# Slot attention: two batches run as two streams half a round apart

## What is computed

```python
Pn = rmsnorm(P, input_norm_w)
k_proj, v_proj = Pn @ Wk.T, Pn @ Wv.T
for _ in range(3):
    sn = rmsnorm(slots, slot_norm_w)
    q_proj = sn @ Wq.T
    scores = jnp.einsum('bkd,bmd->bkm', q_proj, k_proj) * SCALE
    attn = jax.nn.softmax(scores, axis=-2)
    attn = attn / (jnp.sum(attn, axis=-1, keepdims=True) + EPS)
    updates = jnp.einsum('bkm,bmd->bkd', attn, v_proj)
    slots = gru_cell(updates, slots, wih, whh, bih, bhh)
```

## Time and profile before

| What | us |
|---|---|
| Runs (three) | 3412.17, 3408.17, 3413.89 |
| Median | 3412.17 |
| The profiled execution, its own time | 3412.49 |
| Its span, from the first to the last instruction | 3410.7 |
| PE busy in it | 2470.1 (72%) |
| DVE busy | 2040.2 (60%) |
| ACT busy | 1425.7 (42%) |
| Mean granted clock of TensorE | 0.843 of full speed |

### The profile page before, as it was taken

How to read it: one execution, slowest core, us unless ns; L and a number is a source line. 1 busy time by engine, 2 the same in 40 slices (tenths; PEclk the granted TensorE clock), 3 DMA queues, 4 the chain that set the end, 5 groups by cost and what they waited for, 6 DMA issues and landing times. The chain is left out here.

```text
span 3410.7 us, 37710 instructions
## 1 busy us (share of the span) xinstructions
PE 2470.1 (72%) x12065; PEld 1570.8 (46%) x12066; DVE 2040.2 (60%) x4897; ACT 1425.7 (42%) x2245; POOL 423.8 (12%) x228
## 2 busy tenths in 40 slices
PE   2999995363666666654799277877884996899598
PEld 1444443241333333323799145545433884454387
DVE  4666662857777777733465345565654556675377
ACT  1555551113888777861344122122351222266121
POOL 0000000011000000001675120211100111200021
PEclk8999998675777777766899689988886997799799
DMA  1001102043011111001564200000521111531010
GB/s 59 21 24 25 26 17 78 17 131 96 1 26 26 26 26 26 7 1 47 181 202 145 80 0 0 0 0 11 149 51 34 45 31 64 156 86 32 30 42 31
DMA packets 87781, 174.61 MB, mean 51 GB/s; under 512 B 23560, under 2 KB 52240, under 8 KB 84176
## 3 DMA queue, kind: packets, MB, share of 16 engines
q1 hardware_dynamic: 86096, 168.64, 16.9%
q0 software_dynamic: 1536, 4.20, 0.4%
HBM read 133.41 MB, written 38.99 MB: 51 GB/s over the span
## 5 line engine op out<-in xcount | busy, mean ns | idle before, releaser
L1497 ACT ACTIVATE l1a_over_s<-l1a_sc_s,l1a_minus_step_s 128x1024 bf16<-128x1024 f32 x256 | 290.0, 1140 | 3.0 <-DVE l1a_minus_step_s L1371 1.7
L1311 DVE MAX8 l1a_cand_s<-ps 128x8 f32<-128x128 f32 x1024 | 213.2, 282 | 69.0 <-PE ps L1206 65.1
L1239 PE MATMUL ps<-l1a_probs_s,l1h_v_s 128*32 128x256 f32 x1024 | 123.3, 570 | 159.8 <-ACT l1a_probs_s L1505 158.5
L1483 ACT ACTIVATE l1a_sc_s<-ps,l1a_minus_tau_s 128x1024 f32<-128x1024 f32 x128 | 142.0, 1112 | 140.3 <-DVE l1a_minus_tau_s L1340 53.1
L1024 DVE TENSOR_REDUCE l3a_shift_s<-ps 128x1 f32<-128x1024 f32 x128 | 150.1, 1219 | 51.1 <-PE ps L941 51.1
L1206 PE MATMUL ps<-l1h_ka_s,l1h_qa_s 128*128 128x512 f32 x256 | 132.2, 559 | 56.1 <-DVE l1a_cand_s L1311 45.5
L1085 ACT ACTIVATE l3a_probs_s<-ps 128x512 f32<-128x512 f32 x256 | 132.7, 603 | 88.9 <-PE ps L957 88.7
L1962 PE MATMUL ps<-m1e_x_part_s,m1e_up_part_s 128*128 128x256 f32 x1152 | 151.7, 289 | 13.6 <-POOL m1e_up_part_s L2142 12.0
L1962 PEld LDWEIGHTS ps<-m1e_x_part_s,m1e_up_part_s 128*128 128x128 f32 x1152 | 144.4, 196 | 17.0 <-POOL m1e_up_part_s L2142 15.0
L1505 ACT ACTIVATE l1a_probs_s<-ps 128x1024 f32<-128x1024 f32 x128 | 125.7, 1016 | 62.7 <-PE ps L1227 62.7
L646 ACT ACTIVATE l0a_probs_s<-ps 128x1024 f32<-128x1024 f32 x128 | 124.1, 1021 | 53.6 <-PE ps L482 52.0
(11 more groups left out here) (575 smaller groups left out, 5509.8 us busy)
## 6 DMA issues: line engine op xcount, KB each, us to landing
m1e_up_s<-m_up SPq DMA_DIRECT2D x32, 768.0 KB, 4.4
m1e_down_s<-m_down SPq DMA_DIRECT2D x16, 768.0 KB, 4.6
l1h_ka_s<-l_k_parts SPq DMA_DIRECT2D x16, 512.0 KB, 8.0
l3h_ka_s<-l_k_parts SPq DMA_DIRECT2D x16, 512.0 KB, 8.0
l0a_w_s<-l_w SPq DMA_DIRECT2D x16, 384.0 KB, 3.1
m3ew_up_s<-m_up SPq DMA_DIRECT2D x6, 768.0 KB, 4.3
l0a_rden_s<-l0a_rden_rows SPq DMA_DIRECT2D x32, 128.0 KB, 2.9
m_sorted<-ones SPq DMA_DIRECT2D x1, 4096.0 KB, 16.5
```

The lines of the kernel that those rows point to most:

```text
L1239: ins = nc.tensor.matmul(ps[32 * h:32 * h + 32, VALUES, 0:HALF], v[:, n % 2, t, h, :], probs[:, t % 4, h * HALF:(h + 1) * HALF], start=(t ...
L1311: ins = nc.vector.max(cand[:, r, 8 * (c + j * 4):8 * (c + j * 4) + 8], ps[:, A0 + f % 2, c * P:(c + 1) * P])
L1483: nc.scalar.activation(sc[:, r, :], ps[:, PAIR + 2 * (place % 2):PAIR + 2 * (place % 2) + 2, :].rearrange("p a n -> p (a n)"), ACT.Relu, b ...
L1497: nc.scalar.activation(over[:, done % 2, :], sc[:, r, :], ACT.Relu, bias=minus_step[:, r:r + 1], accum_out=total[:, i, r:r + 1]).then_inc( ...
```

## The change

The loop over three rounds is written out as six phases h, where phase h belongs to batch h % 2 and round h // 2. Between the chunks of phase h stand the last three updates, the denominator, the gates and the new state of phase h-1, and then the queries of phase h+1, which is the same batch as h-1. Score banks are 0 and 1 alone, updates 2 and 3, the gates r, z, xn, hn in 4 to 7; queries use 4 and 5, square sums 6, denominators 7. The gates' products with the slots (`state_gates`) are issued apart from those with the updates (`update_gates`), and each gate has semaphores of its own. Squares are made by VectorE instead of ScalarE. The last phase turns batch 0 before the gates of batch 1. The diff, cut:

```diff
     ITERS = 3
+    PHASES = ITERS * B
-    LAG = 3
-    FIRST, SECOND = (0, 1, 5, 6), (2, 3, 4, 7)
+    SCORES, UPDATE, DEN = 0, 2, 7
+    R, Z, XN, HN = 4, 5, 6, 7
+    QUERIES, SQUARES = 4, 6
...
+        def tokens(h):
+            return slice(h % B * NQ, h % B * NQ + NQ)
+
+        def queries_in(h):
+            return 1 <= h and h + 1 < PHASES
...
         @block.tensor
-            with pe.Fori(0, ITERS) as i:
...
+            def scores(h, t):
+                k = NC_ * h + t
+                if t == 0:
+                    pe.wait_ge(q_ready, KC * h + KC)
+                if k >= 2:
+                    pe.wait_ge(exp_done, k - 1)
+                at = (h % B * NC_ + t) * P
+                product(SCORES + k % 2, k_parts, slice(at, at + P), qu_parts, tokens(h)).then_inc(scored, 1)
...
+            def denominator(h):
+                pe.wait_ge(attn_summed, NC_ * h + NC_)
+                if h > 0:
+                    pe.wait_ge(hn_read, KC * h)
+                nc.tensor.matmul(ps[:, DEN, :], ones[:, :], attn_sum[:, :], start=True, stop=True
+                                 ).then_inc(den_made, 1)
...
+            def state_gates(h, m):
+                u = KC * h + m
+                if u > 0:
+                    pe.wait_ge(r_done, u)
+                product(R, weights["whh"], gate(0, m), slot_parts, tokens(h), last=False)
+                pe.wait_ge(den_read, h + 1)
+                if u > 0:
+                    pe.wait_ge(hn_read, u)
+                product(HN, weights["whh"], gate(2, m), slot_parts, tokens(h))
+                if u > 0:
+                    pe.wait_ge(z_done, u)
+                product(Z, weights["whh"], gate(1, m), slot_parts, tokens(h), last=False).then_inc(whh_made, 1)
+
+            def update_gates(h, m):
+                u = KC * h + m
+                pe.wait_ge(upd_ready, h + 1)
+                product(R, weights["wih"], gate(0, m), qu_parts, tokens(h), first=False).then_inc(r_made, 1)
+                if u > 0:
+                    pe.wait_ge(hn_ready, u)
+                product(XN, weights["wih"], gate(2, m), qu_parts, tokens(h)).then_inc(n_made, 1)
+                product(Z, weights["wih"], gate(1, m), qu_parts, tokens(h), first=False).then_inc(z_made, 1)
...
+            for h in range(B):
+                if h > 0:
+                    pe.wait_ge(mean_ready, h)
+                    pe.wait_ge(q_ready, KC * h)
+                square_sums(h)
+                queries(h)
+            for h in range(PHASES):
+                scores(h, 0)
+                if h > 0:
+                    update(h - 1, 5)
+                scores(h, 1)
+                if h > 0:
+                    update(h - 1, 6)
+                    denominator(h - 1)
+                    update(h - 1, 7)
+                scores(h, 2)
+                scores(h, 3)
+                if h > 0:
+                    state_gates(h - 1, 0)
+                    update_gates(h - 1, 0)
+                update(h, 0)
+                if h > 0:
+                    state_gates(h - 1, 1)
+                    update_gates(h - 1, 1)
+                update(h, 1)
+                scores(h, 4)
+                if queries_in(h):
+                    square_sums(h + 1)
+                update(h, 2)
+                scores(h, 5)
+                if queries_in(h):
+                    queries(h + 1)
+                update(h, 3)
+                scores(h, 6)
+                update(h, 4)
+                scores(h, 7)
+            h = PHASES - 1
+            update(h, 5)
+            update(h, 6)
+            denominator(h)
+            update(h, 7)
+            turn(0)
+            for m in range(KC):
+                state_gates(h, m)
+                update_gates(h, m)
+            turn(1)
...
         @block.scalar
+            for h in range(PHASES):
+                for t in range(4):
+                    exponential(h, t)
+                if h > 0:
+                    for m in range(KC):
+                        gates(h - 1, m)
+                if queries_in(h):
+                    root(h + 1)
+                for t in range(4, NC_):
+                    exponential(h, t)
...
         @block.vector
+            def state(h, m):
+                u, tok = KC * h + m, tokens(h)
+                more = h + B < PHASES
+                dve.wait_ge(n_ready, u + 1)
+                own.link(nc.vector.tensor_tensor(slots[:, m, tok], slots[:, m, tok], n_t[:, u % 2, :], ALU.subtract))
+                dve.wait_ge(z_done, u + 1)
+                own.link(nc.vector.tensor_tensor(slots[:, m, tok], slots[:, m, tok], z_t[:, u % 2, :], ALU.mult))
+                nc.vector.tensor_tensor(slots[:, m, tok], slots[:, m, tok], n_t[:, u % 2, :], ALU.add
+                                        ).then_inc(state_done, 1)
+                dve.wait_ge(state_done, u + 1)
+                if more:
+                    own.done(nc.vector.tensor_tensor(sq[:, m, :], slots[:, m, tok], slots[:, m, tok], ALU.mult))
+                    if m == KC - 1:
+                        own.wait()
+                        nc.vector.sem_inc(sq_ready, 1)
+                    dve.wait_ge(whh_made, KC * h + KC)
+                    cut(m, tok, parts_ready)
...
+            for h in range(PHASES):
+                largest(h, 0)
+                if h > 0:
+                    attention(h - 1, 7)
+                largest(h, 1)
+                attention(h, 0)
+                if h > 0:
+                    finish(h - 1)
+                largest(h, 2)
+                attention(h, 1)
+                largest(h, 3)
+                attention(h, 2)
+                if h > 0:
+                    candidate(h - 1, 0)
+                attention(h, 3)
+                if h > 0:
+                    state(h - 1, 0)
+                    candidate(h - 1, 1)
+                    state(h - 1, 1)
+                largest(h, 4)
+                if queries_in(h):
+                    means(h + 1)
+                largest(h, 5)
+                if queries_in(h):
+                    roots_over(h + 1)
+                attention(h, 4)
+                if queries_in(h):
+                    queries(h + 1)
+                largest(h, 6)
+                attention(h, 5)
+                largest(h, 7)
+                attention(h, 6)
```

More of the change, by code:

```diff
@@ L2567, in slot_gru @@
         sq = s.sb("sq", [P, KC, BANK])
-        rs = s.sb("rs", [P, 2, BANK])
-        dev = s.sb("dev", [P, BANK])
+        rs, dev = s.sb("rs", [P, BANK]), s.sb("dev", [P, BANK])
         top = s.sb("top", [P, 8])
@@ new lines, in _ @@
+            act.wait_ge(b_ready, 1)
+            for h in range(B):
+                root(h)
+            for h in range(PHASES):
+                for t in range(4):
+                    exponential(h, t)
+                if h > 0:
+                    for m in range(KC):
+                        gates(h - 1, m)
[3 more added lines that the diff above has]
+                    exponential(h, t)
+            for m in range(KC):
+                gates(PHASES - 1, m)
@@ new lines, in add @@
+            def add(b):
+                dve.wait_ge(turned, b + 1)
+                for t4 in range(2 * b, 2 * b + 2):
+                    rows = x[:, 2 * t4:2 * t4 + 2, :].rearrange("p a n -> p (a n)")
+                    nc.vector.tensor_tensor(rows, rows, ps[:, t4, :], ALU.add).then_inc(added, 1)
+            for h in range(B):
+                if h > 0:
+                    dve.wait_ge(sq_summed, h)
+                for m in range(KC):
+                    own.done(nc.vector.tensor_tensor(sq[:, m, :], slots[:, m, tokens(h)], slots[:, m, tokens(h)], ALU.mult))
+                own.wait()
+                nc.vector.sem_inc(sq_ready, 1)
+                for m in range(KC):
+                    cut(m, tokens(h), parts_ready)
+                if h == 0:
+                    dve.wait_ge(loaded, 32)
+                    nc.vector.tensor_tensor(brz[:, :], bih[:, 0:4], bhh[:, 0:4], ALU.add).then_inc(b_ready, 1)
+                means(h)
+                roots_over(h)
+                queries(h)
@@ L2832, in _ @@
+            h = PHASES - 1
+            attention(h, 7)
+            finish(h)
+            add(0)
+            for m in range(KC):
+                candidate(h, m)
+                state(h, m)
+            add(1)
+            dve.wait_ge(added, 4)
         @block.gpsimd
         def _(pool):
-            with pool.Fori(0, ITERS) as i:
-                for k in range(CHUNKS):
-                    b, t = divmod(k, NC_)
-                    if t == 0:
-                        continue
+            for h in range(PHASES):
+                for t in range(1, NC_):
+                    k = NC_ * h + t
+                    pool.wait_ge(attn_ready, k + 1)
```

351 lines of the change are left out of this document (141 added, 210 removed).

## The result

| | before | after |
|---|---|---|
| Median of four runs each, us | 3410.47 (3408.17 to 3413.89) | 3360.62 (3354.55 to 3362.88) |
| The profiled execution, its own time | 3412.49 | 3360.47 |
| Its span | 3410.7 | 3358.5 |
| The stage, from its first load to that of the next stage | 384.76 | 329.47 |
| PE, DVE, ACT busy | 2470.1, 2040.2, 1425.7 | 2464.4, 2048.2, 1425.8 |

The ratio is 0.9848 [0.9835, 0.9862]: faster, by 50 us in the medians and 52 in the two profiled executions. The forecast was 3359.1 us.

The account below looks back on a forecast made before the run. The prediction took uncovered latencies of one batch as the bound, 90 of 376 us being waiting or low clock. Stage -59.2, holds +2.4 and clock +3.4 made -53.4 from 3412.5: 3359.1 us, 80% range 3339 to 3381.

Parts of the forecast that it names:

- The finish hidden by the state gates: In a steady phase, VectorE's 7.63 us finish is ready at 14.95, before TensorE's state gates end at 15.8.
- A phase: Steady phases 1 to 4: 47.1 us of TensorE work plus new waits of 1.5 and 1.6 us, 50.2 us.
- Named waits: TensorE waits 1.5 us for the squares and 1.6 us for exponential 6 before the next phase's first scores.
- GpSimd's holds: VectorE operations held beside GpSimd additions: query casts 0.6 us per phase, 2.4 us in all; bounds 0 and 10.8.
- The clock: TensorE's clock falls after idle gaps: two falls taken, 3.4 us; bounds none and ten gaps, 17 us.
- Ends: Stage start and finish: first maximum at 2012.6, phase 5 takes 75.5 us, stage ends at 2309.8 instead of 2368.96.
- Busy sums: Sign: VectorE's busy sum unchanged but for moved squares, 12 x 0.69, replacing 6.4 us of ScalarE's.
- The sum: Whole program: stage -59.2, holds +2.4, clock +3.4, together -53.4 us, giving 3359.1 us.
- (A): Rival: TensorE-bound, both new waits vanish through quicker VectorE hand-overs; phase 47.1 us, time 3341 us; chance 0.13.
- (B): Rival: VectorE's order bounds, with held operations, growing gaps and clock falls; phase 56.3 us, time 3377 us; chance 0.20.
- (C): Rival: slower, TensorE stays at the low clock in interleaved phases; at a third of the work 3432 us; chance 0.04.
- (D): Rival: no overlap, late finish delays update gates, 12 us more in each of five phases; about 3412 us; chance 0.03.

Follow-up runs that it names:

- e1_seq: Kernel after the change, but each phase does its own updates, gates and next queries before the other stream's first chunk: 3411.21 us, ratio 0.9993.
- e9_three: Kernel after the change with early reciprocal, tanh ahead of z and earlier first queries of the second stream, square sum kept first: 3346.35 us, ratio 0.9799.
- e3: Kernel after the change without six of GpSimd's seven running additions of attention per phase, one run: 3359.24 us.
- e4: Kernel after the change with VectorE's reciprocal of the root ahead of maximum 5, one run: 3347.43 us.
- e5: Kernel after the change with ScalarE's tanh ahead of the sigmoid of z, one run: 3354.3 us.
- e8: Kernel after the change with early reciprocal, update 2 ahead of the square sum, tanh ahead of z and earlier second stream: 3347.87 us, ratio 0.9813.
- e10: The kernel after the change, unedited, run again on the same chip: 3361.16 us, ratio 0.9846.
- e2: Kernel after the change with only the next square sum and queries moved behind the phase's chunks: 3377.58 us, ratio 0.9898.

## Why the prediction was right

Of its numbers the end is right, and so are most of the steps. The mechanism came out as walked. That the median (3360.62) lies within 1.5 us of the forecast is luck in part: the four runs lie 8 us apart, and the stage ended 2.1 us early while later stages gave 3.2 back.

- *What bounds the kernel: latencies of one batch with nothing of the other to cover them.* Shown by `e1_seq`: the same operations on the same engines and banks without the interleaving give the old time, 0.9993 [0.9983, 1.0003].
- *The finish hidden by the state gates, 0.85 us to spare.* It has 0.90, and the update gates of each interleaved phase wait for nothing.
- *A phase: 47.1 of TensorE + 1.5 + 1.6 = 50.2, and 0.6 of a held cast.* Measured 50.62. The terms: TensorE's work is 47.6 (50.62 less 3.02 of waits; in `e9_three`, where it waits next to nothing, a phase is 47.7), so mis-sized by 0.5; the squares' wait is 1.24, not 1.5; the wait at the start 1.20 without the hold (`e3`), not 1.6; the hold 0.59. The waits are 0.66 shorter mainly because TensorE comes 0.5 later to them, not because the chains are quicker. From a phase's first scores to the square sum it is 34.72 us, walked as 34.6, and from there to the next first scores 15.31 without the hold (`e3`), walked as some 15.6. So the chain takes 50.03, against 50.2. It sets the phase, which is why TensorE's work could be 0.5 off and the phase come out.
- *Named waits.* Both waits are where the walk had them, ended by the squares and by exponential 6. The walk also wrote down "maximum 5, then a reciprocal" and priced the result without seeing that it was an order one could turn round; `e4` shows that this alone made the wait.
- *GpSimd's holds.* "The first state operations are held too, but they then wait for the gates anyway": so it is, 1122 ns in the mean and no cost. The Trainium skill, GPSIMD Engine Reference, says in the table of its section Specifications that the two engines share the SBUF interfaces, with contention where a VectorE instruction runs in a 2-port mode or has two SBUF inputs. The trace agrees for the operation with two such inputs, which took 1.72 us beside an addition; the held cast (1.02) has one, and no row shows whether it ran in a 2-port mode. The 10.8 us to which that rule would have led the sum are not there, since only 0.59 for each phase lies on the path.
- *The clock: two falls, 3.4 us.* One in the phases of the profiled execution, after a wait of 1.78. It cost about 1.6: scores and update took 4.36 us (2235.81 to 2240.17), the same two at full clock 1.47 + 1.32.
- *Ends.* The first maximum starts at 2013.0 (2012.6 predicted). The last phase takes 77.7 us from its first scores to the end of the stage, 75.5 predicted, and the fall of the clock is in it.
- *Busy sums.* VectorE's rose by 8.0 us, 8.3 predicted, which is luck in part: its groups in the stage also show operations that take 9.1 us longer (5.3 the first state operation, 2.4 the query casts, 1.4 attention), and 4.5 less for the last round's cuts into parts, which the new code leaves out. ScalarE's did not fall by the 6.4 us of its squares, since its table loads rose from 12 to 16, at 1.28 us each; the prediction had counted 17 and left them out of this sign.
- *The sum.* With holds and falls the stage was to end at 2309.8 + 5.8 = 2315.6; it ended at 2313.5, 2.1 early. Then 3.2 us were given back in later stages, which no term foresaw. So -52.0 came out for -53.4.

Of the rivals, (A), a phase of 47.1, did not happen here, but its state exists: two turned orders away, in `e9_three`, with 47.73 and the time at 3346 where (A) had 3341. Its reason, quicker hand-overs, was worth only 0.2 us (50.03 against 50.2): what stood in between was order. (B) needed phases of 56.3 and gaps that grow: none grew, and holds overlapped with waits. (C) needed a quarter of each phase at the low clock: in windows of 10 us from 2020 to 2300 it is 1.00 but for the one with the fall, 0.85, and the one behind it, 0.98. (D) needed a late finish: it is in time by 0.90 us.

## What to carry to other kernels

When two streams are laid half a round apart, walk each engine's order once for each result that the other stream is to cover, and look for two things: an instruction whose input is ready but which stands behind one that waits (the reciprocal behind maximum 5, the tanh behind z), and the head of the longest chain, which must not be moved back to fill a gap. Turning two such pairs round was worth 2.9 us a phase here; filling the gap at the head of the chain with other work gave nothing. An operation that is held by another engine costs only what lies on the path: look at what its reader waits for, not at its duration.

## What the runs showed of the hardware

- *A held operation ends shortly after the other engine's addition.* The cast at 2129.28 starts 0.55 us into GpSimd's addition of 1.29 and ends 0.28 after its end; a state operation that started 0.12 into one (2106.21) took 1.72 instead of 0.69 and ended 0.55 after its end. Without the additions the means were the usual ones (427 and 693 ns). The second pair, after:

```profile
2106.09 1.29 POOL L2954 TENSOR_TENSOR g_attn_sum_s<-g_attn_sum_s,g_attn_s 128x512 f32<-128x512 f32 x1 [2.70 <-DVE g_attn_s L2830]
2106.21 1.72 DVE L2864 TENSOR_TENSOR g_slots<-g_slots,g_n_t_s 128x512 f32<-128x512 f32 x1 [0.20 <-ACT g_n_t_s L2764]
```

- *The same gap may or may not cost the clock.* Six profiles have waits of 1.75 to 1.79 us at their phase starts (after, `e5` to `e8`, `e10`), 24 starts in all. Five were followed by work at less than the full clock, the other 19 were not. All waits of 1.20 to 1.24 us at these two places kept it, and all four of 6.30 us in `e2` lost it. The forecast's two rows, 1.99 kept and 2.19 fell, were no threshold. In windows of 2 us, after, around the fall at 2235.81:

```profile
2234.00:2236.00 2.00, 0.22 (x2) 0.22 (x2) 1.93 (x6) 0.78 (x2) 0.47 (x1) 1.00 0.00 0
2236.00:2238.00 2.00, 2.00 (x7) 1.49 (x7) 1.25 (x5) 0.78 (x2) 1.64 (x2) 0.75 0.00 0
2238.00:2240.00 2.00, 2.00 (x3) 0.67 (x2) 1.18 (x4) 0.78 (x2) 1.11 (x2) 0.50 0.01 4
2240.00:2242.00 2.00, 2.00 (x8) 1.43 (x7) 0.00 (x0) 0.00 (x0) 0.59 (x1) 0.90 0.00 0
```

TensorE is busy without a pause in the last three, so the fall comes after the gap, not in it.
